# Layer 0 marks: the keys shown to all partitions by TensorE, the cells cleared from SyncE's queue, every fourth quad compared on ScalarE

## The chip, the core and the metric

The kernel runs on one core of a Trainium2 chip. A core has TensorE (PE, matrix products into PSUM), VectorE (DVE), ScalarE (ACT), GpSimd (POOL) and SyncE (SP); SP, ACT and POOL each have a queue of DMA transfers, which run on the core's 16 DMA engines. The metric is the device time of one execution in microseconds. The kernel before took 3633.55 us (median of three runs, 3632.69 to 3640.02).

## What is computed

A graph of 3125 nodes with 256 features and 50,000 edges, sorted by destination, goes through four layers. Each adds its input back and normalises the rows. Only the first, layer 0, is touched:

```python
gathered = edge_weight[:, None] * x[edge_col]
neigh = jax.ops.segment_sum(gathered, edge_row, num_segments=N_NODES)
w_self, w_neigh = (weight[:D_IN], weight[D_IN:])
out = x @ w_self + neigh @ w_neigh + bias
```

Here `edge_row` is the list `src` and `edge_col` the list `dst`: a source node sums the features of its destinations, each times its edge's weight. Layers 1 to 3 (a graph attention with edge attributes, a graph convolution with two attentions, and three rounds of sums over neighbours with small products) use the same edges.

## The kernel before, in words

Layer 0 does not gather features edge by edge. It makes a matrix of cells in DRAM, `t_w`, with one row for each destination (26 tiles of 128 rows) and one column for each source (3200): a cell holds the summed weight of the edges of one pair of nodes and their count. Products with this matrix give `neigh` for layer 0, and the counts, turned, are kept as the adjacency `t_adj` for later layers. Each step below has its function in the listing.

*Clearing.* The cells are 85.2 MB. ACT's queue writes zeros over them in 13 pieces (`PIECES`, L1401 to L1409), two under way at a time, each counted by `w_zero`.

*Marks.* The edges lie as 392 tiles of 128 (a tile's 128 edges on the partitions), four tiles to a quad, 98 quads. Two edges of a tile that share a pair of nodes must not be scattered one over the other, so every edge first gets the sum over all edges of its quad with the same key (destination × 3200 + source). For that DVE compares: `compare(k)` (L1991 to L1999) takes the quad's 512 keys, the same on all partitions (`wide_key`), against the 128 keys of each of its four tiles, one per partition (`adj_f`), and writes marks of 1 and 0 in bf16 (`same_key`, two buffers). PE multiplies the marks with the values spread by `values_spread` (the count and the weight in three bf16 parts) in `marks(n, k)`, four products of 512 columns per quad, which add up in one PSUM bank per batch. `BATCHES` are of 2, 2, 4, eleven times 8, and 2 quads. After a batch DVE copies the bank (`rows_summed`), PE turns it (`sums_turned`), and DVE writes the sums (`summed`, counted by `w_summed`). Between the first eleven quads DVE does the `early_work` of layer 1.

*How the keys get to all partitions.* DVE makes the keys of all edges in `adj_m` (L1888 to L1890, 98 partitions × 512: partition q holds quad q). SP writes them to DRAM (`t_key`) and loads them back in 49 transfers of two quads each, `two_quads`, to all 128 partitions. A load waits until both quads of its buffer have been compared. The program has a share for ScalarE in the compare, which `FIRST = QUADS` sets to none.

*Scatter.* POOL's `weight_sums` issues 391 indirect DMAs (L777), one for each tile of edges, into `t_w`. They go in groups of eight quads, and inside a group the first tiles of all quads come first. A group waits until the cells that it needs are cleared; an edge tile waits until its quad is summed; and at most eight scatters are under way. `w_landed` counts the quads that have landed.

*Behind the marks.* On SP's queue the rows that layer 1 needs per step follow the key loads (`t_drel`, `t_hi`, `t_lo1`, then 27 copies into `t_lo`, L543). On ACT's queue the first loads (L1421 to L1426) follow the clearing. PE multiplies the nodes' own rows (`own_product`, 25 tiles), and then the pairs: 13 pairs of row tiles of `t_w`, loaded by SP in halves (L572) once their quads have landed (`complete`), each multiplied with `x` (L967) and turned into counts (L942, L945). ACT stages the counts (L1443).

Of the kernel before, what the change touches and what calls it, by code (L numbers as in the profile page):

```python
# [6 lines left out]
P = 128  # L7
N = 3125
NT = 25
NP = NT * P  # L10
E = 50000
ET = 392
EB, EQ = 4, 98
S = ET + NT - 1
# [34 lines left out]
FIRST = QUADS  # L49
# [33 lines left out]
def build(nc, a):  # L83

    with ExitStack() as ctx:
# [141 lines left out]
        same_key = [buf.bitcast(BF16).rearrange("p (u e) -> p u e", u=L0H) for buf in (shared_sb[:, 3200:4224], flat_a[:, 2880:3904])]  # L227
# [21 lines left out]
        no_key = flat_k[0:S - ET, 9 * EB * P:9 * EB * P + P]  # L249
        lo_rows = flat_k[0:SQ, 5216:5472].bitcast(BF16).rearrange("p (b e) -> p b e", b=SB)  # L250
        lo_rows_i = flat_k[0:SQ, 5472:5984].rearrange("p (b e) -> p b e", b=SB).bitcast(I32)
        wide_key = [buf.rearrange("p (h e) -> p h e", h=2) for buf in (shared_sb[:, 2176:2176 + 2 * L0H * P], resid_sb[:, 5120:5120 + 2 * L0H * P])]
        key_gap = flat_a[:, 4224:4224 + 2 * L0H * P].rearrange("p (u e) -> p u e", u=2)
# [34 lines left out]
        t_key = dram("t_key", (S, P))  # L288
# [27 lines left out]
        key_in = [sem(f"key_in{h}") for h in range(2)]  # L316
        in_four, so_far = attr_in + key_in, [16 * len(range(h, PIECES, 2)) for h in range(2)] + [16 * len(range(n, QUADS // 2, 2)) for n in range(2)]
# [9 lines left out]
        def by_layer(name, *counts):  # L327
# [22 lines left out]
                  [("weighted1", 2), ("self_w1", 1), ("weighted2", 2), ("self_w2", 1)], [("diag_clear", 1), ("apart", S // QU), ("gaps", 3 * (S // HU))], [("x1_back", 16), ("x2_back", 16)], [("quad_sum", QUADS), ("own_mm", NT), ("adj_turned", BLOCKS * PAIRS)], [("same_act", QUADS), ("adj_staged", BLOCKS * PAIRS)], [("w_summed", QUADS), ("own_sum", NT)], [("step_mask", EB), ("te", 1), ("adj_rows", 1), ("adj_ev", 1), ("keys", 2), ("pre", 1), ("attr_split", 1)], [("te_ps", 3), ("adj_tp", 1), ("steps_ps", 2), ("steps_ev", 1), ("early_one", 1)],  # L350
# [153 lines left out]
        def _(sp):  # L504
# [18 lines left out]
            sp.wait_ge(*count("key_out", 32))  # L523
            def two_quads(i):

                if i >= 2:
                    sp.wait_ge(*count("same_dve", 2 * i - 2))
                    sp.wait_ge(*count("key_used", 2 * i - 2))
                sp.dma_start(wide_key[i % 2].rearrange("p h e -> p (h e)"), on_each(t_key, i * 2 * L0H, 2 * L0H)).then_inc(key_in[i % 2], 16)

            for i in range(QUADS // 2):
                two_quads(i)

            sp.wait_ge(*count("keys", 2))
            put(t_drel.rearrange("(b q) e -> q b e", b=SB), drow_b, done("key_out"))
            put(t_hi.rearrange("(b q) e -> q b e", b=SB), hi_b, done("rows_out"))
            put(t_lo1[0:S, :].rearrange("(b q) e -> q b e", b=SB), lo_rows, done("rows_out"))
            put(t_lo1[S:S + UN, :], lo_rows[0:UN, 0, :], done("rows_out"))
            put(weights_l1[:, :, 0:D], a["L1_gnn_W"].rearrange("(c p) n -> p c n", p=P), done("ld_w1"))
            sp.wait_ge(*count("rows_out", 48))  # L540
            by_steps = t_lo.rearrange("n (j r) e -> (n j) r e", j=QU)
            for i in range(S // UN + 1):
                sp.dma_start(by_steps[i * UN:(i + 1) * UN], t_lo1[i * UN:(i + 1) * UN, :].unsqueeze(1).to_broadcast([UN, P // QU, P])  # L543
                             ).then_inc(done("lo_out"), 16)
# [11 lines left out]
            sp.wait_ge(*count("same_dve", QUADS))  # L556
            sp.wait_ge(*count("key_used", QUADS))
# [316 lines left out]
        def _(pe):  # L874
# [53 lines left out]

            pe.wait_ge(*count("pre", 1))
            pe.wait_ge(*count("steps_ev", 1))  # L930
# [40 lines left out]
            pe.wait_ge(*count("adj_ev", 1))  # L971
            def marks(n, k):

                kk = k - START[n]
                pe.wait_ge(*count("same_dve", k + 1))
                pe.wait_ge(*count("same_act", k + 1))
                if kk == 0:
                    pe.wait_ge(*count("spread_v", n + 1))
                    if n >= 2:
                        pe.wait_ge(*count("sum_rows", n - 1))  # L980
                for b in range(L0H):
                    mm = pe.matmul(ps[0:32, 4 + n % 2, :], spread_v[n % 2][:, b * WIDE + kk * 32:b * WIDE + kk * 32 + 32], same_key[k % 2][:, b, :],  # L982
                                   start=(kk == 0 and b == 0), stop=(kk == BATCHES[n] - 1 and b == L0H - 1))
                mm.then_inc(done("quad_sum"), 1)
# [408 lines left out]
        def _(act):  # L1393
            act.sem_inc(done("enc_done"), 2)
            act.sem_inc(done("hot_k"), 1)
            act.sem_inc(done("key_used"), FIRST)
            act.sem_inc(done("same_act"), FIRST)
# [3 lines left out]
            act.wait_ge(*count("zeroed", 1))  # L1401
            no_sums = zeros.unsqueeze(1).to_broadcast([P, 4 * NP // W_ZERO, W_ZERO])
            parts_w = t_w.rearrange("(k p n w) o -> k p n (w o)", k=PIECES, p=P, w=W_ZERO // 2)
            for n in range(PIECES + 2):
                if n >= 2:
                    act.wait_ge(attr_in[n % 2], 16 * (n // 2))
                    act.sem_inc(done("w_zero"), 1)
                if n < PIECES:
                    act.dma_start(parts_w[(n - 1) % PIECES], no_sums).then_inc(attr_in[n % 2], 16)  # L1409
            def compare(k):  # L1410

                h = k % 2
                act.wait_ge(key_in[k // 2 % 2], 16 * (k // 4) + 16)
                act.activation(key_gap[:, h, :], wide_key[k // 2 % 2][:, h, :], ACT.Abs, bias=adj_f[:, k * L0H + L0H - 1:k * L0H + L0H], scale=-1.0).then_inc(done("key_used"), 1)
                act.wait_ge(*count("key_used", k + 1))
                act.wait_ge(*count("quad_sum", k - 1))
                act.activation(same_key[h][:, L0H - 1, :], key_gap[:, h, :], ACT.Relu, bias=ones[:, 0:1], scale=-1.0).then_inc(done("same_act"), 1)

            act.wait_ge(*count("attr_split", 1))
            act.wait_ge(*count("adj_ev", 1))  # L1420
            act.dma_start(t_attr.rearrange("(b q) e -> q b e", b=SB), attr_b.rearrange("p b m e -> p b (m e)")).then_inc(done("attr_out"), 16)  # L1421
            act.dma_start(rows[:, :, :], a["rows"]).then_inc(done("ld_rows"), 16)
            act.dma_start(vecs[:, :, :], a["vecs"]).then_inc(done("ld_vecs"), 16)
            act.dma_start(weights[:, :, 0:D], a["L0_gnn_weight"].rearrange("(c p) n -> p c n", p=P)).then_inc(done("ld_w0"), 16)
            act.dma_start(cols[:, :, :], a["x_cols"].rearrange("(c p) n -> p c n", p=P)).then_inc(done("ld_x"), 16)
            act.dma_start(hrows[:, :, 0:D], a["x_pad"].rearrange("(t p) d -> p t d", p=P)).then_inc(done("ld_xh"), 16)  # L1426
            for k in range(FIRST, QUADS):
                compare(k)
# [23 lines left out]
            act.wait_ge(*count("rows_out", 48))  # L1452
# [370 lines left out]
        def _(dve):  # L1823
# [65 lines left out]
            link(dve.memset(no_key, -1.0))  # L1889
# [101 lines left out]
            def compare(k):  # L1991

                h = k % 2
# [34 lines left out]
            for n in range(len(BATCHES)):  # L2028
                values_spread(n)
                for k in range(START[n], START[n + 1]):  # L2030
                    compare(k)
# [323 lines left out]
            def first_layer_nodes():  # L2355
# [31 lines left out]
                dve.wait_ge(*count("key_out", 48))  # L2387
                dve.wait_ge(*count("rows_out", 48))
# [265 lines left out]
```

## Time and profile before

| | us |
|---|---|
| median of three runs | 3633.55 |
| profiled execution | 3642.44 |
| its span | 3640.7 |
| PE, DVE, POOL, ACT busy | 2939.2, 2400.9, 1719.4, 1422.3 |
| granted TensorE clock, mean | 0.893 |

The span is the time from the first to the last instruction of the profiled execution. An engine's busy time is the time in which it worked on instructions, waits left out; the granted clock is the share of TensorE's full speed that the chip let it have. The first three stages (marks, own products, pairs) take some 723 us of the span.

### The profile page before, as it was taken

How to read it: one execution, taken by the hardware profiler on the slowest of the kernel's cores; microseconds unless marked ns; L12 is line 12 of the kernel's file. 1: busy time of each engine (PE TensorE's matmuls, PEld its weight loads, DVE VectorE, ACT ScalarE, POOL GpSimd, SP SyncE). 2: the span in 40 equal slices, each digit the busy share in tenths (PEclk: the TensorE clock that was granted, in tenths of full speed). 3: DMA queues.
4: the chain of work that ended last, by engine and by line, in shares of the span. 5: the costliest groups of instructions: out<-in, count | busy, mean ns of one | idle time of the engine just before them, and what ended most of it. 6: DMA issues, size and time to landing. Idle time of an engine off the chain costs nothing. (4 is left out here: it accounts for less than half of the span.)

```text
span 3640.7 us, 59184 instructions
## 1 busy us (share of the span) xinstructions
PE 2939.2 (81%) x15077; PEld 1873.4 (51%) x15078; DVE 2400.9 (66%) x5574; ACT 1422.3 (39%) x3005; POOL 1719.4 (47%) x1731
## 2 busy tenths in 40 slices
PE   4556999989999588978769986676986559999896
PEld 2113444567777434448654433564433347587675
DVE  7556332459988898973779987468986773333434
ACT  0000222259998466651016663303664350310402
POOL 3777775007555676402777773376777400000000
PEclk6667999989999799988979997887998769999998
DMA  9998888749898555427841110694445234133241
GB/s 399 404 378 255 289 307 278 255 120 248 261 270 248 172 176 181 151 78 281 227 133 28 27 27 14 220 316 136 140 129 183 65 101 135 47 114 104 73 144 36
DMA packets 399986, 651.00 MB, mean 179 GB/s; under 512 B 129821, under 2 KB 274934, under 8 KB 392690
## 3 DMA queue, kind: packets, MB, share of 16 engines
q1 hardware_dynamic: 244441, 367.78, 32.0%
q0 software_dynamic: 72144, 145.54, 13.5%
q10 hardware_dynamic: 83213, 135.59, 10.1%
q8 instruction: 66, 1.08, 0.1%
q14 instruction: 122, 1.00, 0.1%
HBM read 468.36 MB, written 183.90 MB: 179 GB/s over the span
## 5 line engine op out<-in xcount | busy, mean ns | idle before, releaser
L1501 ACT ACTIVATE onehot<-iota,drel 128x128 f32<-128x128 f32 x1248 | 381.6, 388 | 683.3 <-PE ps L1204 344.2
L1204 PE MATMUL ps<-shared_sb,onehot 128*128 128x264 f32 (+1 forms) x1600 | 552.5, 441 | 92.5 <-DVE accum L2293 87.4
L2293 DVE TENSOR_TENSOR accum<-accum,ps 128x264 f32 (+1 forms) x1248 | 526.0, 422 | 11.4 <-issue 4.0
L777 POOL DMA_INDIRECT t_w<-early_sb x391 | 414.7, 1061 | 164.0 <-issue 96.4
L1204 PEld LDWEIGHTS ps<-shared_sb,onehot 128*128 128x128 f32 x1600 | 257.5, 198 | 386.6 <-issue 244.1
L794 POOL TENSOR_SCALAR onehot<-iota,carry_d 98x512 bf16<-98x512 f32 x28 | 44.7, 1603 | 784.9 <-PE ps L1281 646.0
L1264 PE MATMUL ps<-counts_r,h_hi 128*128 128x512 f32 (+1 forms) x1050 | 321.5, 387 | 12.2 <-DVE h_lo L2556 12.2
L813 POOL DMA_INDIRECT shared_sb<-table,src_x x272 | 261.0, 960 | 112.8 <-issue 75.2
L1264 PE MATMUL ps<-counts_r,h_lo 128*128 128x512 f32 (+1 forms) x1050 | 312.4, 379 | 0.0
L813 POOL DMA_INDIRECT rows<-table,src_x x184 | 181.9, 988 | 180.6 <-DMA table<-score_sb 92.2
L860 POOL DMA_INDIRECT resid_sb<-table,src_x x224 | 211.7, 945 | 89.0 <-issue 57.3
L2370 DVE TENSOR_TENSOR accum<-accum,ps 128x512 f32<-128x512 f32 (+1 forms) x156 | 103.8, 667 | 221.4 <-PE ps L967 220.0
L2279 DVE TENSOR_TENSOR shared_sb<-shared_sb,ps 128x256 f32<-128x256 f32 x512 | 211.5, 413 | 43.7 <-DMA shared_sb<-table,src_x 24.6
L1125 PE MATMUL ps<-score_sb,onehot 128*128 x832 | 219.4, 407 | 19.6 <-issue 16.6
L1264 PEld LDWEIGHTS ps<-counts_r,h_hi 128*128 128x128 f32 x1050 | 195.9, 190 | 54.1 <-issue 12.6
L1264 PEld LDWEIGHTS ps<-counts_r,h_lo 128*128 128x128 f32 x1050 | 193.2, 190 | 39.1
L813 POOL DMA_INDIRECT score_sb<-table,src_x x168 | 170.4, 1014 | 75.4 <-issue 48.2
L813 POOL DMA_INDIRECT resid_sb<-table,src_x x144 | 136.4, 947 | 142.3 <-DMA t_resid<-resid_sb 87.4
L967 PE MATMUL ps<-resid_sb,score_sb 128*128 128x512 f32 (+1 forms) x364 | 187.9, 597 | 0.0
L1504 ACT ACTIVATE onehot<-onehot,ones 128x1024 f32<-128x1024 f32 x156 | 179.2, 1149 | 5.1
L1125 PEld LDWEIGHTS ps<-score_sb,onehot 128*128 128x128 f32 x832 | 150.6, 191 | 55.6 <-issue 25.7
L982 PE MATMUL ps<-shared_sb,resid_sb 128*32 128x512 bf16 x196 | 80.6, 557 | 116.5 <-DVE shared_sb L1998 110.6
(432 smaller groups left out, 5929.8 us busy)
## 6 DMA issues: line engine op xcount, KB each, us to landing
t_w<-onehot ACTq DMA_DIRECT2D x13, 6400.0 KB
accum<-t_hot SPq DMA_DIRECT2D x208, 256.0 KB
shared_sb<-t_adj SPq DMA_DIRECT2D x53, 640.0 KB, 9.5
resid_sb<-t_w SPq DMA_DIRECT2D x13, 1664.0 KB
t_aside<-rows POOLq DMA_DIRECT2D x40, 512.0 KB
resid_sb<-t_w SPq DMA_DIRECT2D x13, 1536.0 KB
score_sb<-t_w SPq DMA_DIRECT2D x12, 1664.0 KB
shared_sb<-t_w SPq DMA_DIRECT2D x12, 1536.0 KB
```

The lines of the kernel that those rows point to most:

```text
L777: pool.indirect_dma_start(t_w, bass.IndirectOffsetOnAxis(ap=w_x[:, j:j + 1], axis=0), w_pair[:, j, :], None).then_inc((moved + gath)[n % ( ...
L813: pool.indirect_dma_start(to[:, u, 0:w], None, tab, bass.IndirectOffsetOnAxis(ap=src_x[:, step:step + 1], axis=0)).then_inc(landing[0], 16)
L860: pool.indirect_dma_start(x_rows[n % (RG[1] // HU)][:, u, :], None, table[1], bass.IndirectOffsetOnAxis(ap=src_x[:, n * HU + u:n * HU + u ...
L967: mm = pe.matmul(ps[:, m % 6, at:at + now.stop - now.start], lhs, w_cells[2 * h + t % 2][0:EQ if t == NT else P, from_half, 0], start=(t = ...
L1125: mm = pe.matmul(ps[:, 4 + j, 0:GW], hot, hrows[:, bass.ds(at[q * QU + j], 1), :], start=True, stop=True)
L1204: pe.matmul(ps[:, RING[(HU * h + u) % len(RING)], 0:w], onehot[:, h % 2 * HU + u, :], around[g][place(g, i, h)][:, u, 0:w], start=True, st ...
L1264: mm = pe.matmul(ps[:, 2 * (i % 3) + f, 0:w], part[:, t, f * P:(f + 1) * P], whole_counts[at % WORK][:, c, 0:w], start=(t == 0 and part is ...
L1501: last = act.activation(onehot[:, h % 2 * HU + u, :], iota[:, 0:P], ACT.Abs, bias=drel[:, bass.ds(step + u, 1)], scale=-1.0)
L1504: act.activation(onehot[:, pair, :], onehot[:, pair, :], ACT.Relu, bias=ones[:, 0:1], scale=-1.0).then_inc(oh_ready, 1)
L2279: dve.tensor_tensor(v, of_src, now_w[:, u, 0:H].unsqueeze(2).to_broadcast([P, H, D // H]), ALU.mult).then_inc(msg_ready, 1)
L2293: dve.tensor_tensor(to, to, bank.unsqueeze(1), ALU.add).then_inc(step_acc, 1)
L2370: dve.tensor_tensor(to, to, bank, ALU.add).then_inc(done("w_sum"), 1)
```

## The change

- PE shows the keys. DVE splits `adj_m` into two float32r parts (`key_parts`, their sum is the key), and `keys_shown(k)` multiplies each with column k of an identity, the same column for all 128 outputs, so that a PSUM bank (k modulo 4) holds quad k's 512 keys on all partitions. Two quads are shown early, a third behind `adj_ev`, and then each `marks(n, k)` begins with quad k + 3. `t_key`, its two writes and its 49 loads are gone.
- DVE and ScalarE compare from PSUM. `SHARE = 4`: quads 3, 7, 11, ... 95 (24 of 98) are ScalarE's, which has a mark buffer of its own; DVE's two alternate over its 74. ScalarE takes |key − own key| for each of the four tiles (four Abs) and then max(0, 1 − that) over all 2048 columns (one Relu), its gap now in bf16.
- SP clears the cells. The 13 pieces go out on SP's queue behind `adj_rows`, and in their middle (behind the issue of piece 6) come the step rows and the 27 copies (`step_rows_out`), ahead of the key loads' old place. `rows_out` now counts `t_drel` too.
- ScalarE's first loads stand behind its fourth quad (at k = 16), no longer behind the clearing.

```diff
-FIRST = QUADS
+SHARE = 4
+        def on_act(k):
+            return k % SHARE == SHARE - 1
+        def compared(k):
+            return count("same_act", k // SHARE + 1) if on_act(k) else count("same_dve", k - k // SHARE + 1)
+        def same_slot(k):
+            return same_key[2] if on_act(k) else same_key[(k - k // SHARE) % 2]
+        def slot_before(k):
+            return k - SHARE if on_act(k) else k - 2 - (on_act(k - 1) or on_act(k - 2))
...
 @block.sync
-            put(t_key[0:ET, :].rearrange("(q b) e -> q b e", b=EB), adj_m, done("key_out"))
-            put(t_key[ET:S, :], no_key, done("key_out"))
...
-            for i in range(QUADS // 2):
-                two_quads(i)
+            sp.wait_ge(*count("zeroed", 1))
...
+            for n in range(PIECES + 2):
+                if n >= 2:
+                    sp.wait_ge(attr_in[n % 2], 16 * (n // 2))
+                    sp.sem_inc(done("w_zero"), 1)
+                if n < PIECES:
+                    sp.dma_start(parts_w[(n - 1) % PIECES], no_sums).then_inc(attr_in[n % 2], 16)
+                if n == PIECES // 2:
+                    step_rows_out()
...
-            sp.wait_ge(*count("same_dve", QUADS))
-            sp.wait_ge(*count("key_used", QUADS))
+            sp.wait_ge(*count("quad_sum", QUADS))
             sp.wait_ge(*count("w_summed", QUADS))
...
 @block.tensor
+            def keys_shown(k):
+                if k >= 4:
+                    pe.wait_ge(*compared(k - 4))
+                for m in range(2):
+                    mm = pe.matmul(ps[:, k % 4, :], pick_row[0:EQ, k:k + 1].to_broadcast([EQ, P]), key_parts[m][0:EQ, :], start=(m == 0), stop=(m == 1))
+                mm.then_inc(done("key_ps"), 1)
             pe.wait_ge(*count("pre", 1))
+            pe.wait_ge(*count("key_parts", 1))
+            for k in range(2):
+                keys_shown(k)
             pe.wait_ge(*count("steps_ev", 1))
...
 def marks(n, k):
+                if k + 3 < QUADS:
+                    keys_shown(k + 3)
-                pe.wait_ge(*count("same_dve", k + 1))
-                pe.wait_ge(*count("same_act", k + 1))
+                pe.wait_ge(*compared(k))
...
 @block.scalar
 def compare(k):
+                act.wait_ge(*count("key_ps", k + 1))
+                if k >= SHARE:
+                    act.wait_ge(*count("quad_sum", slot_before(k) + 1))
+                    act.wait_ge(*count("same_act", k // SHARE))
+                for u in range(L0H):
+                    at = k * L0H + u
+                    act.activation(key_gap[:, u, :], ps[:, k % 4, :], ACT.Abs, bias=adj_f[:, at:at + 1], scale=-1.0).then_inc(done("key_used"), 1)
+                act.wait_ge(*count("key_used", L0H * (k // SHARE) + L0H))
+                act.activation(same_slot(k)[:, :, :], key_gap[:, :, :], ACT.Relu, bias=ones[:, 0:1], scale=-1.0).then_inc(done("same_act"), 1)
+            for k in range(QUADS):
+                if k == 16:
+                    first_loads()
+                if on_act(k):
+                    compare(k)
...
 @block.vector
+            dve.wait_ge(*count("adj_rows", 1))
+            dve.tensor_copy(pick_row[:, :], ident[:, :])
+            keys_of = adj_m.rearrange("p b e -> p (b e)")
+            link(dve.tensor_copy(key_parts[0][0:EQ, :], keys_of))
+            dve.tensor_tensor(key_parts[1][0:EQ, :], keys_of, key_parts[0][0:EQ, :], ALU.subtract).then_inc(done("key_parts"), 1)
...
 def compare(k):
-                h = k % 2
-                dve.wait_ge(key_in[k // 2 % 2], 16 * (k // 4) + 16)
-                if k >= 2:
-                    dve.wait_ge(*count("quad_sum", k - 1))
-                for u in range(L0H if k < FIRST else L0H - 1):
-                    last = dve.tensor_scalar(same_key[h][:, u, :], wide_key[k // 2 % 2][:, h, :], adj_f[:, k * L0H + u:k * L0H + u + 1], None, ALU.is_equal)
+                dve.wait_ge(*count("key_ps", k + 1))
+                if slot_before(k) >= 0:
+                    dve.wait_ge(*count("quad_sum", slot_before(k) + 1))
+                for u in range(L0H):
+                    last = dve.tensor_scalar(same_slot(k)[:, u, :], ps[:, k % 4, :], adj_f[:, k * L0H + u:k * L0H + u + 1], None, ALU.is_equal)
                 last.then_inc(done("same_dve"), 1)
```

## Rows read from the trace of the kernel before

**Rows 1.** Busy time by stretch; columns: stretch, length, engines' busy us (instructions), clock, DMA share, GB/s.
```profile
100.00:270.00 170.00, 93.06 (x250) 27.05 (x251) 99.38 (x251) 0.00 (x0) 133.50 (x119) 0.67 1.00 393
...
43.27:339.03 295.76, 161.47 (x453) 47.17 (x453) 197.81 (x489) 0.00 (x0) 210.21 (x178) 0.67 0.95 366
...
365.00:700.00 335.00, 322.32 (x1307) 154.53 (x1305) 108.57 (x160) 92.75 (x161) 184.88 (x193) 0.98 0.85 293
```

**Rows 2.** Timeline of PE; columns: start, length, engine, line, operation, idle time before and releaser.
```profile
289.74 1.89 PE L982 MATMUL ps<-shared_sb,resid_sb 128*32 128x512 bf16 x4 [8.13 <-DVE shared_sb L1998]
...
319.60 1.04 PE L982 MATMUL ps<-shared_sb,resid_sb 128*32 128x512 bf16 x4 [0.94 <-DVE shared_sb L1998]
...
364.64 0.22 PE L942 MATMUL ps<-ident_h,resid_sb 128*128 128x128 f16 x1 [0.79 <-DMA shared_sb<-t_w]
```

**Rows 3.** Groups of DVE, 43.27 to 339.03: busy, mean ns; idle before, releasers.
```profile
L1998 DVE TENSOR_SCALAR shared_sb<-shared_sb,early_sb 128x512 bf16<-128x512 f32 x100 | 42.6, 487 | 79.3 <-DMA shared_sb<-t_key 78.8 <-PE ps L982 0.3
L1998 DVE TENSOR_SCALAR accum<-shared_sb,early_sb 128x512 bf16<-128x512 f32 x100 | 41.5, 473 | 0.1
L1998 DVE TENSOR_SCALAR shared_sb<-resid_sb,early_sb 128x512 bf16<-128x512 f32 x96 | 41.5, 492 | 17.7 <-DMA resid_sb<-t_key 16.2 <-PE ps L982 1.4
L1998 DVE TENSOR_SCALAR accum<-resid_sb,early_sb 128x512 bf16<-128x512 f32 x96 | 40.5, 481 | 0.2
L2014 DVE COPY resid_sb<-ps 32x512 f32<-32x512 f32 x15 | 10.1, 672 | 0.8 <-PE ps L982 0.8
```

**Rows 4.** Timeline of the DMA issues on the queues of ACT and SP.
```profile
2.81 228.90 ACTq L1409 DMA_DIRECT2D t_w<-onehot  x13
24.52 1.64 SPq L506 DMA_DIRECT2D t_key<-score_sb  x2
272.66 0.64 ACTq L1421 DMA_DIRECT2D t_attr<-score_sb  x1
...
280.63 0.58 ACTq L1426 DMA_DIRECT2D score_sb<-in_x_pad  x1
333.91 19.08 SPq L543 DMA_DIRECT2D t_lo<-t_lo  x27
...
658.12 0.32 SPq L572 DMA_DIRECT2D resid_sb<-t_w  x1
```

**Rows 5.** POOL's scatters: durations min/median/max, first and last start; then the timeline.
```profile
L777 POOL DMA_INDIRECT t_w<-early_sb x391: 954/959/5131, 63.7 to 608.5; - x196
...
79.92 1.67 POOL L777 DMA_INDIRECT t_w<-early_sb  x1 [11.10 <-DVE early_sb L2023]
...
91.38 0.96 POOL L777 DMA_INDIRECT t_w<-early_sb  x1 [0.30 <-issue]
```

**Rows 6.** Timeline of DVE, the first compare and a copy from PSUM.
```profile
43.27 1.67 DVE L1998 TENSOR_SCALAR shared_sb<-shared_sb,early_sb 128x512 bf16<-128x512 f32 x4 [4.74 <-DMA shared_sb<-t_key]
...
60.27 0.67 DVE L2014 COPY resid_sb<-ps 32x512 f32<-32x512 f32 x1
60.87 0.91 DVE L1951 TENSOR_SCALAR with_first<-shared_sb 104x128 f32<-104x128 f32 x3
```

**Rows 7.** The chain that ended last, a stretch of float32r matmuls of a later layer.
```profile
3029.37 23.18 PE ps L1264 x100
```

**Rows 8.** Costliest groups of the page: an f32 matmul of the pairs, a wide Relu.
```profile
L967 PE MATMUL ps<-resid_sb,score_sb 128*128 128x512 f32 (+1 forms) x364 | 187.9, 597 | 0.0
L1504 ACT ACTIVATE onehot<-onehot,ones 128x1024 f32<-128x1024 f32 x156 | 179.2, 1149 | 5.1
```

**Rows 9.** Timeline of ACT: three reads of a PSUM bank.
```profile
368.44 1.70 ACT L1443 ACTIVATE early_sb<-ps 128x512 f16<-128x512 f32 x3
```

**Rows 10.** Busy time of POOL alone in two stretches.
```profile
91.00:340.00 249.00, 196.47 (x172) 0.70 0.94 355
340.00:609.50 269.50, 203.78 (x213) 0.98 0.86 288
```

**Rows 11.** Groups of PE, 0 to 400 us: the turned sums of the batches.
```profile
L992 PE MATMUL ps<-ident,resid_sb 32*128 32x32 f32 x60 | 8.6, 275 | 0.8 <-DVE resid_sb L2014 0.8
```

More of the change, by code:

```diff
@@ L248, in build @@
         weights_l1 = flat_k[:, 3456:3456 + 2 * GW].rearrange("p (c w) -> p c w", c=2)
-        no_key = flat_k[0:S - ET, 9 * EB * P:9 * EB * P + P]
         lo_rows = flat_k[0:SQ, 5216:5472].bitcast(BF16).rearrange("p (b e) -> p b e", b=SB)
         lo_rows_i = flat_k[0:SQ, 5472:5984].rearrange("p (b e) -> p b e", b=SB).bitcast(I32)
-        wide_key = [buf.rearrange("p (h e) -> p h e", h=2) for buf in (shared_sb[:, 2176:2176 + 2 * L0H * P], resid_sb[:, 5120:5120 + 2 * L0H * P])]
-        key_gap = flat_a[:, 4224:4224 + 2 * L0H * P].rearrange("p (u e) -> p u e", u=2)
+        key_parts = [over(f"key_part{m}", "shared_sb", 2176 + m * EB * P, [EB * P]) for m in range(2)]
+        pick_row = over("pick_row", "resid_sb", 5120, [P])
+        key_gap = flat_a[:, 4224:4224 + 2 * L0H * P].bitcast(BF16).rearrange("p (u e) -> p u e", u=L0H)
         ring = {"gcn": shared_sb[:, 0:HOLD * GRP * CW // 2].bitcast(F16).rearrange("p (r c w) -> p r c w", r=HOLD, c=GRP)}
@@ L315, in build @@
         attr_in = [sem(f"attr_in{h}") for h in range(2)]
-        key_in = [sem(f"key_in{h}") for h in range(2)]
-        in_four, so_far = attr_in + key_in, [16 * len(range(h, PIECES, 2)) for h in range(2)] + [16 * len(range(n, QUADS // 2, 2)) for n in range(2)]
+        in_four, so_far = attr_in + [sem(f"attr_in{h}") for h in range(2, 4)], [16 * len(range(h, PIECES, 2)) for h in range(2)] + [0, 0]
         adj_in = [sem(f"adj_in{r}") for r in range(HOLD)]
@@ L531, in _ @@
-            for i in range(QUADS // 2):
-                two_quads(i)
[L534 to L544, printed above, removed]
+            def step_rows_out():
+                sp.wait_ge(*count("keys", 2))
+                put(t_drel.rearrange("(b q) e -> q b e", b=SB), drow_b, done("rows_out"))
+                put(t_hi.rearrange("(b q) e -> q b e", b=SB), hi_b, done("rows_out"))
+                put(t_lo1[0:S, :].rearrange("(b q) e -> q b e", b=SB), lo_rows, done("rows_out"))
+                put(t_lo1[S:S + UN, :], lo_rows[0:UN, 0, :], done("rows_out"))
+                put(weights_l1[:, :, 0:D], a["L1_gnn_W"].rearrange("(c p) n -> p c n", p=P), done("ld_w1"))
+                sp.wait_ge(*count("rows_out", 64))
+                by_steps = t_lo.rearrange("n (j r) e -> (n j) r e", j=QU)
+                for i in range(S // UN + 1):
+                    sp.dma_start(by_steps[i * UN:(i + 1) * UN], t_lo1[i * UN:(i + 1) * UN, :].unsqueeze(1).to_broadcast([UN, P // QU, P])
+                                 ).then_inc(done("lo_out"), 16)
@@ new lines, in _ @@
+            sp.wait_ge(*count("zeroed", 1))
+            no_sums = zeros.unsqueeze(1).to_broadcast([P, 4 * NP // W_ZERO, W_ZERO])
+            parts_w = t_w.rearrange("(k p n w) o -> k p n (w o)", k=PIECES, p=P, w=W_ZERO // 2)
+            for n in range(PIECES + 2):
[6 more added lines that the diff above has]
+                    step_rows_out()
@@ L1395, in _ @@
             act.sem_inc(done("hot_k"), 1)
-            act.sem_inc(done("key_used"), FIRST)
-            act.sem_inc(done("same_act"), FIRST)
             for h in range(UN // QU):
                 act.sem_inc(hot_kept[h], 16)
[L1401 to L1409, printed above, removed]
@@ L1410, in compare @@
-            def compare(k):
-                h = k % 2
[L1413 to L1424, printed above, removed]
@@ new lines, in first_loads @@
+            def first_loads():
+                act.wait_ge(*count("attr_split", 1))
+                act.wait_ge(*count("adj_ev", 1))
+                act.dma_start(t_attr.rearrange("(b q) e -> q b e", b=SB), attr_b.rearrange("p b m e -> p b (m e)")).then_inc(done("attr_out"), 16)
+                act.dma_start(rows[:, :, :], a["rows"]).then_inc(done("ld_rows"), 16)
+                act.dma_start(vecs[:, :, :], a["vecs"]).then_inc(done("ld_vecs"), 16)
+                act.dma_start(weights[:, :, 0:D], a["L0_gnn_weight"].rearrange("(c p) n -> p c n", p=P)).then_inc(done("ld_w0"), 16)
+                act.dma_start(cols[:, :, :], a["x_cols"].rearrange("(c p) n -> p c n", p=P)).then_inc(done("ld_x"), 16)
+                act.dma_start(hrows[:, :, 0:D], a["x_pad"].rearrange("(t p) d -> p t d", p=P)).then_inc(done("ld_xh"), 16)
@@ L2030, in _ @@
                 for k in range(START[n], START[n + 1]):
-                    compare(k)
+                    if not on_act(k):
+                        compare(k)
                     if n > 0 and k < START[n] + 2:
```

25 lines of the change are left out of this document (6 added, 19 removed).

## The prediction

> **What bounds the kernel now.** I read the busy time by stage, then DVE's groups of one stage, then the queues. Three early stages matter. The marks (compares on DVE, products of the marks on PE) last from the first compare at 43.27 us to 339.03, where the products of the nodes' own rows begin; at 364.6 the products by pairs of tiles follow [rows 1, 2]. In the pair stage PE is busy 322 of 335 us at the full level (granted 0.98): PE bounds it, and it starts when the own products are done. In the marks no engine is full: DVE 197.8 of 295.8 us, PE 161.5 at a granted clock of 0.67, ScalarE 0 [rows 1]. The groups say why: the four forms of the compare (L1998) are busy 42.6 + 41.5 + 41.5 + 40.5 = 166.1 us, and before them DVE waits 78.8 + 16.2 = 95.0 us for the loads from t_key [rows 3]. So 95 of DVE's 98 idle us are those loads, 49 of 512 KB (25.7 MB by shape), the same rows sent to all 128 partitions, while ACT's queue writes 13 pieces of zeros (85.2 MB by t_w's shape) [rows 4]: together they fill the DMA engines (share 1.00, 393 GB/s from 100 to 270 us) [rows 1]. The transfers bound the marks. Beside all this POOL issues 391 scatters of weights from 63.7 to 608.5 us [rows 5]. The marks reach the end of the program by two ways: the pair stage starts 25 us after them, and its pairs 11 and 12 need nearly all scatters landed.
>
> **The change, part by part.**
>
> *The loads of keys* go: 2 writes and 49 loads on SP, and 95.0 us of DVE's idle time. What is late next is DVE itself.
>
> *The compares on DVE.* 24 of the 98 quads (every fourth) go to ScalarE, so DVE does 74 × 4 = 296 compares, now from PSUM. The trace has no compare from PSUM. The nearest row is the copy of 512 columns from PSUM, 672 ns [rows 3], and the next instruction starts 0.60 us after it (60.27 to 60.87) [rows 6]; from SBUF a compare costs 166.1 / 392 = 0.42. I take 0.60: source, width and 4-byte element are the copy's. Sum: 296 × 0.60 = 177.6 us where 166.1 stood. The ends: 0.42 gives 125.4, and no overlap between neighbours, 0.67, gives 198.9.
> The Trainium skill (VectorE: DVE Perf Modes, Why PSUM operands drop a tier) speaks against this part: a PSUM operand takes an fp32 operation out of the doubled rate. The two rows above agree, 0.60 against 0.42. By its clock alone, one column in each cycle of 0.96 GHz (an estimate from that page), 296 × 0.533 = 158 us, and the marks would be 20 us shorter than I say.
>
> *The rest of DVE in the stage* stays: 197.8 − 166.1 = 31.7 us of sums, spreads and the early work of layer 1. The three operations that make the key parts are each about as long as the 0.67 us above or shorter, and stand before the first compare, where DVE sat idle 4.74 us [rows 6]; PE shows the first two quads there as well. I let the first compare start 0.7 us later, at 44.0.
>
> *PE.* It gains 98 × 2 matmuls of 512 columns beside the 98 × 4 of the marks. A quad of marks takes 1.04 us at the upper level (2.4 GHz) and 1.89 at the lower (1.2 GHz) [rows 2]. The float32r matmuls of L1264 come every 23.18 / 100 = 0.23 us [rows 7], so a shown quad costs 0.46, and 0.95 at the lower level if it follows the marks' ratio. Four quads are 6.0 us at the upper level and 11.4 at the lower. DVE's turn for the same four is 3 × 2.40 plus about 0.8 for sums and spreads: 8.0. So PE keeps up at the upper level alone. In the marks before it was at the lower one more often than not (0.67 granted), with 161 of 296 us busy; in the pair stage, nearly always busy, it was granted 0.98 [rows 1]. At 6.0 of 8.0 us it lies between them, and whenever it falls to the lower level it has work without a gap, which is what it had in the pair stage. I charge 6 us for stretches at the lower level. Bound: if these products cost what the plain f32 ones of L967 do (187.9 / 364 = 0.52) [rows 8], four quads cost 8.3 us, and PE and DVE are level.
>
> *ScalarE* was idle. Its quad: four Abs from PSUM at 1.70 / 3 = 0.57 [rows 9], one Relu over 2048 columns, at most twice the 1149 ns of 1024 [rows 8]; with two handovers about 4.9 us. It has one mark buffer, so it starts when PE has used the last one: 0.5 (shown) + 4.9 + 1.0 (marks) = 6.4 of the 8.0 us, hidden with 1.6 to spare. That cover goes once: its six first loads now stand behind its fourth quad instead of at 272.7 us, where issuing them took until 281.2, 8.5 us [rows 4]. PE waits for the next ScalarE quad, and DVE behind it runs out of buffers: 5 us.
>
> *SyncE* takes the 13 pieces of zeros and, in their middle, the 5 loads and writes and 27 copies of the step rows. Zeros started at 2.81 us; now they wait for the keys, ready when t_key was first written, at 24.5 [rows 4]. POOL's first group needs three pieces: 3 × 6.55 MB at 393 GB/s = 50 us, so at 75 instead of 63.7; but its fifth scatter waits for the sums of quads 4 to 7, at 79.9 before [rows 5] and about 84 now (8 DVE quads at 2.40 against 10 at 1.67). The later start is hidden. All zeros and ScalarE's loads, 85.2 + 9.7 MB (x twice, rows, attributes, weights, by shape) at 393 GB/s, take 241 us, so they are done at 266, or 285 if the 27 copies (19.1 us to issue [rows 4]) hold the zeros up for their whole length. SP's first pair loads are queued behind the last piece. They landed 11.6 us after the copies' issue (353.0 to 364.6) [rows 2, 4], so they land at 278 to 297; PE is done with the own products 25 us after the marks. I charge 1.7 us. In the kernel before, SP issues the 27 copies right before the pair loads; that goes, and is worth under 1 us, as PE waited 0.79 there [rows 2].
>
> *POOL* is not edited, but its scatters get shorter. From 91 to 340 us it was busy 196.5 us for 172 of them, 1.14 each; from 340 on 203.8 for 213, 0.96 each, one every 269.5 / 213 = 1.265 us [rows 10]. The surplus, 172 × 0.185 = 32 us, falls beside the compares, and the four from 79.92 to 91.38 took 11.5 us instead of 5.1 [rows 5]. With compares from PSUM I expect none of it, as the scatters from 340 on run beside DVE's sums from PSUM (L2370). So: 84 + 387 × 1.265 = 574, with a few us for DVE's other copies 577, against 609.5. Pair 11 loads at 658.1 [rows 4], 47 us after the last scatter may have landed; 33 more make 80 us by which the pair stage can move forward before POOL holds it.
> On this the Trainium skill (SBUF — State Buffer, Who interferes with whom) says that a DVE operation in a two-port mode holds the port pair it shares with GpSimd for its whole length, and that one with a single SBUF input outside those modes does not. The rows of both stretches agree; by this rule the 38 us come back in full.
>
> **Sum.** 44.0 + 177.6 + 31.7 + 3 (the idle time left without the key loads) + 5 + 6 = 267.3, against 339.0: the marks end 71.7 us earlier, the pair stage 70. POOL's cap of 80 isn't reached. What follows hangs on the pair stage, so all of it arrives: the profiled 3642.4 (span 3640.7 plus 1.7 around it) becomes 3572.4. That execution is 8.9 us above the median of the three runs, 3633.55; so I predict 3563.5.
>
> **The rivals.**
> - *PE paces the marks* (the lower level for half of them, or costlier products). All at the lower level: 44.0 + 2.4 + 98 × (1.89 + 0.95) + 8.6 for the turned sums [rows 11] = 333: a gain of 6, 3627.5, no change that can be told. Half: some 38, 3596. For it: 0.67 granted in the marks. Against: PE's load rises by half.
> - *DVE's compares don't overlap* (0.67): 21 us more, 3585. The 0.60 rests on a copy, not on a compare with an operand per partition.
> - *The zeros end late.* Should the DMA engines give the 355 GB/s of 91 to 340 us [rows 10]: 24.5 + 267 + 19 = 311, pair loads landed at 322: a gain of 42, 3591.
> - *The other side: POOL is starved.* If compares from PSUM held POOL as those from SBUF did from 79.92 to 91.38 (2.87 us each) [rows 5], then, with DVE busy 94% of the stage, the 183 us from 84 to 267 hold 64 scatters, the other 323 take 409, and POOL ends at 676. Pair 11 then loads at 678, not 658: 20 us slower, 3653. It decides from 2.3 us per scatter on (656 − 267 leaves room for 307, so 80 in 183 us). Against: the scatters from 340 on, beside sums from PSUM.
> - *It doesn't do what it says* would be a start no earlier for the pairs; that is the first rival at its full size.
>
> **How the numbers follow.** Forecast (gain 55 to 80) 0.50; PE half slow 0.13; no overlap 0.11; zeros late 0.08; more than 80 (neither 5 nor 6 lost, no charge for the pairs) 0.05; PE slow throughout 0.05; POOL starved 0.08. Anything within 7.3 us (0.2%) can't be told from no change. Faster 0.87, same 0.05, slower 0.08. The range runs from 3547 (the cap of 80 and 6 us for what isn't priced) to 3606 (a gain of 28, PE slow for more than half); it leaves the last two cases out and a little on either side.
>
> **What would show it.** Right: no DVE wait on a DMA in the marks; 296 compares 0.60 us apart; the first own product near 267 us; PE granted 0.85 or more there; scatters at 0.96 throughout, the last near 577; pair 0 about 25 us after the marks. Wrong: PE quads at 2.8 us; DVE waiting for quad sums; scatters above 2 us; SP's first pair load well after the last sum; a PE gap ahead of pair 11.

## The result, and the profile after

The changed kernel takes 3583.88 us (median of four runs, 3576.91 to 3589.78), the kernel before 3635.20 in the same comparison: ratio 0.9861, 95% interval 0.9846 to 0.9875. That is 51 us faster. 70 were forecast; 3583.9 lies inside the range and 20 us above the predicted 3563.5. The profiled execution is the fastest of its four (3576.91, span 3575.1), so below, places on its time axis are compared with those of the profile before, and total times by medians. In the views, a place is in us from the start of the span.

Busy time of the changed kernel by stretch: the marks, and 335 us of the pair stage (columns as in [rows 1]).

```profile
41.59:290.62 249.03, 190.84 (x647) 69.63 (x646) 230.90 (x393) 106.13 (x120) 159.86 (x162) 0.86 0.98 363
316.00:651.00 335.00, 325.18 (x1336) 156.15 (x1335) 115.76 (x165) 92.89 (x166) 200.60 (x209) 1.00 0.87 299
```

Against [rows 1] the marks are 249.0 us long, not 295.8, and VectorE is busy 230.9 of them (93%), where it was 197.8 of 295.8. Its groups in that stretch:

```profile
L2026 DVE TENSOR_SCALAR shared_sb<-ps,early_sb 128x512 bf16<-128x512 f32 x148 | 100.2, 733 | 3.5 <-PE ps L947 3.5
L2026 DVE TENSOR_SCALAR accum<-ps,early_sb 128x512 bf16<-128x512 f32 x148 | 100.2, 732 | 13.1 <-PE ps L1009 13.0
L2042 DVE COPY resid_sb<-ps 32x512 f32<-32x512 f32 x15 | 10.1, 676 | 2.6 <-PE ps L1009 2.4
```

The 95 us of waiting for t_key [rows 3] are gone (4.7 of them stood ahead of the first compare [rows 6], so 90 in this stretch). What stands there now is work: 296 compares take 200.4 us, 0.677 each (0.66 from one start to the next, 2.64 for four). One wait of 10.23 us is the largest part of the 13.0; the rows of ScalarE below show where it comes from. TensorE's timeline, two quads of marks with the next keys shown ahead of them, then the first product of the own rows and the first pair:

```profile
200.15 0.73 PE L947 MATMUL ps<-key_part,pick_row 98*128 98x512 f32 x2
200.81 1.04 PE L1009 MATMUL ps<-shared_sb,resid_sb 128*32 128x512 bf16 x4
...
203.63 1.04 PE L1009 MATMUL ps<-accum,resid_sb 128*32 128x512 bf16 x4 [0.76 <-DVE accum L2026]
...
290.62 24.72 PE L1034 MATMUL ps<-weights,shared_sb 128*128 128x256 f32 x100 [0.36 <-DVE early_sb L2051]
315.86 0.25 PE L966 MATMUL ps<-ident_h,resid_sb 128*128 128x128 f16 x1 [0.52 <-DVE shared_sb L2075]
```

The own products start at 290.62, 48.4 us earlier than at the end of the marks in [rows 1], the pairs at 315.86, 48.8 earlier than in [rows 2]. In the marks TensorE waits mostly for VectorE's compares (total us, times, longest):

```profile
PE ps L1009 <- DVE accum L2026: 23.7, 24, 3.5
PE ps L1009 <- DVE shared_sb L2026: 22.4, 23, 3.0
PE ps L1009 <- ACT resid_sb L1436: 7.4, 1, 7.4
```

VectorE waits 16.6 us for TensorE (13.0 + 2.4 + 1.2), 10.23 of it in that one wait. ScalarE, at its first loads (the lines with ACTq are DMA issues):

```profile
92.55 2.42 ACT L1434 ACTIVATE accum<-ps,early_sb 128x512 bf16<-128x512 f32 x4 [11.97 <-PE ps L947]
95.00 2.00 ACT L1436 ACTIVATE resid_sb<-accum,ones 128x2048 bf16<-128x2048 bf16 x1
95.06 0.62 ACTq L1442 DMA_DIRECT2D t_attr<-score_sb  x1
95.71 1.19 ACTq L1443 DMA_DIRECT2D rows<-in_rows  x1
...
107.87 6.90 ACTq L1447 DMA_DIRECT2D score_sb<-in_x_pad  x1
114.89 2.42 ACT L1434 ACTIVATE accum<-ps,early_sb 128x512 bf16<-128x512 f32 x4 [17.89 <-issue]
```

and VectorE at the end of that:

```profile
124.36 0.75 DVE L2026 TENSOR_SCALAR accum<-ps,early_sb 128x512 bf16<-128x512 f32 x1 [10.23 <-PE ps L1009]
```

The six issues took from 95.06 to 114.77, each longer than the one before. They are the same six that took 8.5 us in [rows 4]. While it issues, ScalarE compares nothing (its hold, below): TensorE, which takes the quads in order, waits 7.4 us for ScalarE's quad, and VectorE for a mark buffer. SyncE's queue:

```profile
123.20 26.79 SPq L520 DMA_DIRECT2D t_drel<-accum  x1
150.04 8.31 SPq L520 DMA_DIRECT2D t_hi<-accum  x1
158.39 11.20 SPq L520 DMA_DIRECT2D t_lo<-score_sb  x2
...
177.12 18.07 SPq L545 DMA_DIRECT2D t_lo<-t_lo  x27
195.31 73.13 SPq L556 DMA_DIRECT2D t_w<-onehot  x6
304.19 0.37 SPq L585 DMA_DIRECT2D resid_sb<-t_w  x1
```

The first pair load goes only at 304.19, behind the last piece of zeros, 13.6 us after the own products began. GpSimd's scatters (columns as in [rows 5]):

```profile
L790 POOL DMA_INDIRECT t_w<-early_sb x391: 952/958/3387, 77.3 to 581.5; - x196
L790 POOL DMA_INDIRECT t_w<-early_sb x391 | 379.6, 971 | 172.3 <-issue 94.0 <-SPq L554 47.2 <-DMA t_w<-early_sb 27.6
```

They start 14 us later than before and end 27 us earlier. The longest, 3.39 us, lies beside two operations of layer 1's early work that read and write SBUF:

```profile
86.90 2.28 DVE L2018 TENSOR_TENSOR shared_sb<-shared_sb,score_sb 104x2048 f32<-104x2048 f32 x1
89.21 1.23 DVE L2068 CAST score_sb<-shared_sb 104x2048 bf16<-104x2048 f32 x1
```

```profile
87.17 3.39 POOL L790 DMA_INDIRECT t_w<-early_sb  x1 [0.30 <-issue]
```

### The profile page after: what moved, and what is told of

The parts are those of the page before. It is cut to its first block and busy times, and to the rows that moved or that the text cites. A ratio compares the mean times of both kernels' runs of the same rounds, so it can differ in the third digit from the quotient of the medians.

```text
span 3575.1 us, 59355 instructions
## 1 busy us (share of the span) xinstructions
PE 2961.2 (83%) x15273; PEld 1895.3 (53%) x15274; DVE 2435.7 (68%) x5480; ACT 1527.0 (43%) x3125; POOL 1683.7 (47%) x1731
## 5 line engine op out<-in xcount | busy, mean ns | idle before, releaser
L790 POOL DMA_INDIRECT t_w<-early_sb x391 | 379.6, 971 | 172.3 <-issue 94.0
L1141 PE MATMUL ps<-accum 128*128 128x100 bf16 x2496 | 168.9, 224 | 0.0
```

Source lines behind the costliest of these rows:

```text
L790: pool.indirect_dma_start(t_w, bass.IndirectOffsetOnAxis(ap=w_x[:, j:j + 1], axis=0), w_pair[:, j, :], None).then_inc((moved + gath)[n % ( ...
L1141: mm = pe.matmul(out, hot, src_b8[:, m, :] if k == 0 else src_b[:, m, :, :], start=False, stop=(m == 2 and (j % 2 == 1 if k == 0 else j == ...
```

## The experiments

All ten kernels build on the changed one. Each is judged by places of its trace (first compare, first own product, first pair) and, but for experiment 7, by its median against the kernel before, run on the same chip. The experiments ran on three chips, so their medians are compared with each other only through these ratios. In the code, `...` stands for lines left out.

**1. VectorE does all compares.**

```
def on_act(k):
-    return k % SHARE == SHARE - 1
+    return False
...
```

> ScalarE compares nothing; VectorE compares all 98 quads from PSUM, keys still shown by TensorE. Theory (VectorE's compares from PSUM set the marks): 392 x 0.66 = 259 us in place of 296 x 0.66 = 195, less the 10 us in which ScalarE's loads held the marks: first own product at 344 in place of 290.6, no sooner than in the kernel before (339), and a time of 3637, ratio to before 1.00. Rival (TensorE paces the marks, by its lower clock and two matmuls per quad): the first own product stays at 280 to 291 and the time at 3574 to 3584.

Measured: 3632.47, ratio 0.999 (0.9981 to 1.0): no change against before. Its first own product and first pair:

```profile
339.29 10.97 PE L1034 MATMUL ps<-weights,shared_sb 128*128 128x256 f32 x36 [0.36 <-DVE early_sb L2052]
...
364.59 0.25 PE L966 MATMUL ps<-ident_h,resid_sb 128*128 128x128 f16 x1 [0.52 <-DVE shared_sb L2076]
```

The first pair is where it was before the change (364.64). VectorE is busy 292.1 of 296 us and waits 2.4 for TensorE: 265.4 us of compares have replaced 166.1 of compares and 95 of waiting. So showing the keys by TensorE, with all that goes with it, gains nothing by itself; the gain comes only when ScalarE takes its quarter as well. What that quarter would gain with the keys still loaded was not run. The forecast of 344 for the first own product was 5 us too high.

**2 to 4. The first loads on SyncE; the zeros from the start; both.**

```
# loads: on SyncE's queue, not ScalarE's
                 if n == PIECES // 2:
                     step_rows_out()
+                    first_loads()
...
# zeros: SyncE no longer waits for the keys
-            sp.wait_ge(*count("adj_rows", 1))
```

> The six first loads are issued by SyncE behind the step rows, not by ScalarE before its fifth quad. Theory (the hold costs the marks 10 to 13 us, but the zeros, whose last piece lands at 304, let no pair load go sooner): first own product at 278 to 281 in place of 290.6, first pair still at 311 to 319, time within 4 us of the changed kernel (3580 to 3588). Rival (the hold counts in full): first pair at 304, time 3572. Second rival (VectorE makes the hold good with its two other buffers): first own product at 289 to 291, nothing else moves.

> SyncE no longer waits for the keys before the first piece of zeros (4 us in place of 23.9); all else as in the changed kernel. Theory (zeros are late but hidden behind the own products by less than 1 us): last piece lands at about 284, pair loads before 297, first pair at 315 to 316 as before: time 3583 to 3586. Rival (zeros beside the first loads of the program push the first compare back, as transfers then share the DMA engines): first compare at 43 to 45 in place of 41.6 and the time 2 to 4 us up.

> First loads on SyncE and zeros from the start, together. Theory (hold and zeros are two bounds one behind the other): first own product at 278 to 281, pair loads landed before it ends, first pair at 303 to 306, time 3571 to 3574, 10 us below either alone. Rival (the hold alone counts): the same time as with the loads on SyncE alone.

Measured: loads alone 3580.92, ratio 0.9849 (0.9835 to 0.9863); zeros alone 3588.24, 0.9868 (0.9848 to 0.9887); both 3570.24, 0.9814 (0.9799 to 0.983). The first own product and first pair with the loads moved:

```profile
278.30 21.96 PE L1046 MATMUL ps<-weights,shared_sb 128*128 128x256 f32 x89 [0.36 <-DVE early_sb L2050]
...
310.00 0.27 PE L978 MATMUL ps<-ident_h,resid_sb 128*128 128x128 f16 x1 [7.37 <-DMA shared_sb<-t_w]
```

and with both edits:

```profile
280.94 19.29 PE L1045 MATMUL ps<-weights,shared_sb 128*128 128x256 f32 x75 [0.36 <-DVE early_sb L2049]
...
306.15 0.25 PE L977 MATMUL ps<-ident_h,resid_sb 128*128 128x128 f16 x1 [0.52 <-DVE shared_sb L2073]
```

The loads alone bring the own products 12.3 us forward, and 7.37 of it is given back at once: the pair loads, behind the zeros, are late. With the zeros started earlier too, the pair loads go at 282.33, not 299.35, and that wait is gone. The marks with both edits (columns as in [rows 1]):

```profile
42.00:280.90 238.90, 186.24 (x646) 68.34 (x645) 230.75 (x393) 106.13 (x120) 153.01 (x157) 0.89 0.96 358
```

VectorE's idle time in them falls from 18.1 us (249.0 − 230.9) to 8.2 (238.9 − 230.7). So ScalarE's hold cost the marks 10 us. The zeros were hidden behind the own products with less than 1 us to spare, by an estimate: loads that go at 304.19 and take the 10.65 from issue to first pair of the run with the loads alone land at 314.8, and TensorE is done with the own products at 315.3. The zeros alone don't help: the first compare started at 42.73 and the first pair came at 318.56, 2.7 later than in the changed kernel and 2.5 later than expected, a difference that the times don't separate. The first compare came only 0.3 ahead of the rival's 43 to 45, so the rival isn't ruled out. Of these three only the two edits together lie clear of the changed kernel's interval (0.9846 to 0.9875).

**5. ScalarE compares every third quad** (with both edits).

```
-SHARE = 4
+SHARE = 3
```

> As with both edits (loads on SyncE, zeros from the start), and ScalarE compares every third quad: 32, VectorE 66. Theory: VectorE has 264 x 0.68 = 179 us and 33 of other work, but ScalarE's one mark buffer sets the pace: about 6.4 us from one of its quads to the next, 32 x 6.4 = 205 us from 46 on, sums behind it: first own product at 255 to 262 in place of 281. The pair loads then come too late again (issued at 282, landed 10 to 11 us later): first pair at 291 to 295 in place of 306, time 3556 to 3561. Rival (the zeros don't bound): first pair at 281 to 287, time 3547 to 3553. Rival (ScalarE's quad takes longer, TensorE waits in order for it): first own product at 281 or later, time 3570 or more.

Measured: 3563.93, ratio 0.979 (0.9773 to 0.9806). The first own product comes at 266.44, 4 us later than expected, the first pair at 291.69, as expected, after a wait of 1.35 for t_w. The time is 3 us above the forecast, and its interval overlaps that of both edits without the third quad (0.9799 to 0.983): the 14.5 us by which the first pair comes sooner don't all show in the medians.

**6. One matmul for each shown quad.** The keys' second part is left out, so the marks are those of rounded keys.

```
-                for m in range(2):
+                for m in range(1):
...
```

> The changed kernel with one matmul for each shown quad (the second part of the keys is left out, so keys are rounded). Theory (TensorE doesn't pace the marks): first own product at 289 to 292, time 3576 to 3590. Rival (TensorE paces them): 98 matmuls of 0.4 us less, marks 15 to 40 us sooner; the time up to 5 us less, as the pair loads land at 315.

Measured: 3586.82, ratio 0.9865 (0.985 to 0.988), as the changed kernel; first own product at 292.28. A whole matmul for each quad less moves nothing. The granted clock of the marks was lower here, 0.79 against 0.86, and still TensorE waited longer for VectorE's compares, 56.8 us against 46.1: TensorE does not pace the marks.

**7. Compares with a constant** (with both edits; all marks are zero).

```
...
-  ps[:, k % 4, :], adj_f[:, k * L0H + u:k * L0H + u + 1], None, ALU.is_equal)
+  ps[:, k % 4, :], 7.0, None, ALU.is_equal)
```

> As with both edits, and VectorE compares with a constant instead of a column of adj_f (marks are then all zero). First theory (the operand for each partition makes the compare longer than the 0.60 of the copy): four compares take 2.40 to 2.45 in place of 2.73, first own product near 262. Second theory (any such operation on 512 columns from PSUM, written as bf16, takes 0.66 to 0.68): 2.7 and 281 as before.

VectorE's groups in the marks:

```profile
L2024 DVE TENSOR_SCALAR shared_sb<-ps 128x512 bf16<-128x512 f32 x148 | 91.3, 672 | 3.5 <-PE ps L958 3.5
L2024 DVE TENSOR_SCALAR accum<-ps 128x512 bf16<-128x512 f32 x148 | 91.3, 672 | 2.6 <-PE ps L1020 2.5
```

One compare lasts 672 ns, as long as the copy of [rows 3], and four take 2.40 from start to start: 0.60. With the operand for each partition it is 732 and 0.66. The first own product comes at 263.68, against 280.94. The first theory holds, the second is out; this ran once, so only its trace is used.

**8. Compares from SBUF** (with both edits). ScalarE copies each shown row of keys, VectorE compares all 98 quads.

```
...
-  same_slot(k)[:, u, :], ps[:, k % 4, :], adj_f[...]
+  same_slot(k)[:, u, :], keys_sb[:, k % 2, :], adj_f[...]
```

> As with both edits, but ScalarE only copies each shown row of keys from PSUM to SBUF, and VectorE compares all 98 quads from there. Theory (the PSUM source is what a compare pays for: 0.42 from SBUF; and compares from SBUF lengthen GpSimd's scatters): VectorE 392 x 0.42 + 33 = 198 us, first own product at 242 to 250; scatters 1.14 us each beside the compares, 0.97 behind them, the last near 600; first pair at 291 to 295 for the pair loads, and TensorE waits 10 to 25 us ahead of the pairs that need the last scatters; time 3562 to 3585. Rival (the scatters were long for the load on the DMA engines, not for the compares): 0.97 throughout, last scatter at 575 to 580, time 3553 to 3560.

Measured: 3673.76, ratio 1.0099 (1.0083 to 1.0114), slower than before the change. The marks were even shorter than expected (first own product 236.82, 5 us sooner; a compare busy for 0.42). The scatters did far worse:

```profile
L802 POOL DMA_INDIRECT t_w<-early_sb x391: 954/958/13532, 58.2 to 691.1; - x196
```

VectorE about two sums, and GpSimd in the same 25 us:

```profile
122.87 0.67 DVE L2035 COPY resid_sb<-ps 32x512 f32<-32x512 f32 x1
123.47 1.65 DVE L2019 TENSOR_SCALAR accum<-resid_sb,early_sb 128x512 bf16<-128x512 f32 x4
125.05 0.24 DVE L2043 TENSOR_REDUCE early_sb<-ps 128x32 f32<-128x96 f32 x1
125.22 0.21 DVE L2044 CAST early_sb<-ps 128x32 f16<-128x32 f32 x1
125.32 1.65 DVE L2019 TENSOR_SCALAR shared_sb<-resid_sb,early_sb 128x512 bf16<-128x512 f32 x4
...
136.50 0.67 DVE L2035 COPY resid_sb<-ps 32x512 f32<-32x512 f32 x1
```

```profile
112.13 13.33 POOL L802 DMA_INDIRECT t_w<-early_sb  x1 [0.30 <-DVE early_sb L2044]
125.76 11.18 POOL L802 DMA_INDIRECT t_w<-early_sb  x1 [0.30 <-DVE early_sb L2044]
```

A long scatter ends when VectorE does something from PSUM: at 125.46 right behind the sum of 125.05 and its cast, at 136.94 inside the copy of 136.50. So do all ten that take over 9 us; but not at the first chance, as the one that ended at 125.46 had sat through the copy of 122.87. What in those pauses lets it through is not shown. From 84 to 250 us GpSimd got 35 scatters through; the last of the 391 starts at 691. SyncE waits 133.6 us, in 17 pieces, for scatters to land ahead of its pair loads, and TensorE, whose first pair started at 282.56, stands idle 113.7 us in ten pieces of the pair stage. This is the prediction's rival of the starved GpSimd, with its mechanism and a larger price (3673.76 against its 3653), and it belongs to compares from SBUF, which the change gave up. The kernel before compared from SBUF too, but VectorE stood idle for a third of its marks. Of its 172 scatters from 91 to 340 us, the 57 that met no compare took 1.03 each, the other 115 1.25.

**9. The same, the copy at every second 4-byte word.**

```
+  keys_sb = [buf.rearrange("p (e two) -> p e two", two=2)[:, :, 0] for buf in ...]
```

> As with compares from ScalarE's copy in SBUF (a scatter beside them took up to 13.5 us), but the copy lies at every second 4-byte word. Theory (a compare holds GpSimd's scatters only at its fast rate of 0.42, which needs neighbouring words): compares at 0.6 or more apart, scatters 0.97, the last at 575 to 585; marks end at 310 to 340, time 3605 to 3635. Rival (any compare with SBUF source holds the scatters): the last scatter past 640, time above 3660.

Measured: 3675.46, ratio 1.0107 (1.0091 to 1.0122). The stride didn't slow the compare (1.65 for four, as in experiment 8), so the theory's condition never came about; the scatters took up to 13.33 us again:

```profile
L802 POOL DMA_INDIRECT t_w<-early_sb x391: 954/958/13334, 58.3 to 686.8; - x196
```

Whether it is the rate or the source that holds them stays open.

**10. Two mark buffers for ScalarE, the step rows' copies on its queue** (with every third quad).

```
-            return k - SHARE if on_act(k) else ...
+            return k - 2 * SHARE if on_act(k) else ...
...
```

> ScalarE compares every third quad and has two mark buffers; the 27 copies of the step rows are issued by ScalarE behind its last compare, so SyncE's zeros end sooner. Theory: VectorE alone paces the marks, 42.4 + 264 x 0.677 + 33 + 3 = 257 for the first own product (266.4 with one buffer), pair loads issued at 262 to 270, first pair at 283 (291.7 before); but the last scatter still starts at 578, so pair 11's first load goes at 582 as it did with one buffer, TensorE waits some 8 us longer ahead of it, and the time stays at 3559 to 3565. Rival (the scatters don't hold the pairs yet): all 8 us arrive, time 3554 to 3557. Second rival (TensorE's order of quads paces the marks): first own product stays at 263 to 267.

Measured: 3563.17, ratio 0.9794 (0.9781 to 0.9807): nothing beyond experiment 5. First own product 266.32, where the theory had 257. The pair loads do go sooner (267.28, not 281.21), but TensorE reaches them no sooner. ScalarE no longer waits for its own buffer. VectorE is busy 210 of 224.7 us; my 3 us of idle time were 14, most of it waits for TensorE: 4.8 us ahead of the copies of a batch, 4.2 ahead of the turned sums, 3.4 for a mark buffer. That is the second rival's place for the first own product, and in part its reason, though VectorE is at 94%. In both kernels pair 11's first load goes at 582.5, and SyncE waits for scatters ahead of it (5.6 us here, 7.8 in experiment 5); TensorE comes to that pair without a wait. As the pairs started no sooner, whether the scatters would hold earlier ones was not put to the test.

## Why the prediction was right, and where 20 us went

**The mechanism** holds: transfers bounded the marks, VectorE bounds them now, and what the marks gain reaches the pair stage whole (48.4 at the own products, 48.8 at the first pair) and the end (51.3 by the medians).

**The sum**, term by term against the changed kernel's trace:

| term | forecast | measured |
|---|---|---|
| first compare | 44.0 | 41.6 |
| 296 compares | 177.6 | 200.4 |
| other work of VectorE | 31.7 | 30.5 |
| idle: left over, loads, TensorE's clock | 3 + 5 + 6 | 18.1 |
| first own product | 267.3 | 290.6 |

The step that failed in size is "I take 0.60: source, width and 4-byte element are the copy's". The copy's row was the right row for the source, and experiment 7 gives 0.60 for a compare without the operand for each partition; that operand adds 60 ns, 296 times: 17.8 us. Counting busy time, as the table does, it is 22.8: the compares with a constant are busy 182.6 us, 0.617 each, so 5.0 us of it would have come without the operand. It was the second rival (0.67, 3585), for another reason than overlap: neighbours overlap by 0.07 as the copy did. That its 3585 lies within 2 us of the measured time is in part luck, as the other terms missed by −2.4, −1.2 and +4.1.
In the prediction an estimate by the clock alone, from the Trainium skill (VectorE: DVE Perf Modes, Why PSUM operands drop a tier), gave 0.533 for a compare; the trace has 0.66, and the measurement decides.

**ScalarE's first loads** were put at 5 us, from issues that took 8.5 when the zeros were done; they took 19.7 beside the zeros, and the marks lost 10 (experiments 2 to 4). On SyncE's queue, behind its copies, the same six took 8.3 (experiment 2), so the load on the DMA engines alone (share 0.98 there, 1.02 here) doesn't price them; what does is not shown. **TensorE's low clock** was charged 6; with the loads gone, 8.2 us of all idle time are left for that charge and the 3 together. The granted clock is 0.86, as the forecast's condition had it. **TensorE's price** for a shown quad was too low (0.66 from start to start at the full level, 0.46 forecast), and it doesn't matter (experiment 6). At the lower level the marks' ratio makes 0.84 of the 0.46, not the 0.95 that the first rival took; its own sum would have been some 323, not 333. **ScalarE's quad** takes 4.45 of the 4.9.

**The zeros.** The pair loads were to land at 278 to 297. They were issued at 304. SyncE's four step-row writes took 46 us to issue (123.20 to 169.59), where the forecast counted only the 27 copies; before the change these four took 2.1 us, from 328.92 on. SyncE issued no zeros from 123 to 195, and from 170 to 195 the DMA engines moved 156 GB/s, where it had been 404 from 123 to 150. The third rival, zeros late at 355 GB/s, was thus true: the marks had 363 (first view of the result), which by its own sum gives 305 (24.5 + 261 + 19). How much of the delay the writes, the copies and the load each made is not shown; with the copies off the queue the pair loads go 13.9 us sooner (experiment 10 against 5). The late zeros cost nothing only because the marks were late as well: at the forecast's 267 the pairs would have waited some 23 us for them, an estimate (304.19 + 10.65 against 267 + 25; experiment 2 shows 7.37 of it).

**GpSimd**: 0.97 a scatter against 0.96 forecast, last start at 581.5 against an end of 577. Right, and for the reason given (experiment 8). The 11.5 us for four scatters, from which the rival of the starved GpSimd took its 2.87 each, were not the compares' alone: VectorE did early work there too (2.28 us from 82.52, 1.21 from 86.57), and the changed kernel keeps scatters of 2.38 and 3.39 us beside the early work.
The rule cited in the prediction from the Trainium skill (SBUF — State Buffer, Who interferes with whom), by which a VectorE operation in a two-port mode holds the port pair that it shares with GpSimd, agrees in direction with both: 0.97 beside compares from PSUM, up to 13.53 us beside those from SBUF. No run here shows which mode a compare was in, and experiment 9 could not tell the mode from the source.

**Beyond the marks** the profiled pair differs by another 17 us: from the first pair to the last pair load 325.1 us against 332.4, and 9.4 us behind it. Over the kernels here, 8 and 9 apart, the first figure lies between 320.6 and 333.6, without order by edit: 325.1 and 320.6 in the two where TensorE was granted 1.00 in that stretch (the changed kernel and experiment 6), 329.2 to 333.6 where it was granted 0.98. No cause in the edits is shown, so I count it as scatter; the medians' 51.3 is the first pair's 48.8 and little else.

## What to carry to other kernels

When a wait for transfers goes, price each operation that takes its place by a row with the same operands, not only the same source and width: 60 ns on 296 compares was the largest error here. An issue that is moved must be priced by what is under way at its new place: six issues took 8.5 us behind the zeros and 19.7 beside them. And look at what the idle time was doing for others: here GpSimd's scatters went through while VectorE stood idle, and compares from SBUF without those pauses made the kernel slower (experiment 8).

## What the runs showed of the hardware

- A VectorE compare of 512 f32 columns from PSUM: 0.60 us from start to start with a constant (experiment 7), 0.66 with a column as operand (the changed kernel); from SBUF 0.40 with the column (1.58 for four), also at a stride of two words (experiments 8 and 9).
- A GpSimd scatter among such SBUF compares, one behind the other, took up to 13.53 us instead of 0.96; the ten that took over 9 us ended during or right behind an operation of VectorE from PSUM, though not always the first one (experiment 8).
- With the DMA engines full (share 1.02 from 95 to 115 us, zeros under way), six issues on ScalarE's queue took 0.62, 1.19, 1.63, 3.51, 5.71 and 6.90 us (the changed kernel); behind the copies on SyncE's queue the six took 8.3 in all (experiment 2). One write of step rows took 26.79 us to issue behind zeros on SyncE's queue, and 0.40 in the kernel before.
